# Row maxima from the high halves, four heads in four banks, and an attention order made from a model of bank times

## What is computed

```python
x = L0_attn_X
x = x + 0.5 * _L0_ffn_ref(_layernorm(x, axis=-1), ...)
x = x + _L0_attn_ref(_layernorm(x, axis=-1), ...)
x = x + 0.5 * _L0_ffn_ref(_layernorm(x, axis=-1), ...)
...
scores = jnp.einsum('bhqd,bhkd->bhqk', Q, K) / jnp.sqrt(jnp.float32(D_HEAD))
scores = jnp.where(causal, scores, jnp.float32(-jnp.inf))
A = jax.nn.softmax(scores, axis=-1)
AV = jnp.einsum('bhqk,bhkd->bhqd', A, V)
```

## Time and profile before

| | us |
|---|---|
| median of 3 runs | 2673.28 |
| lowest and highest | 2671.97, 2674.62 |
| span of the profiled execution | 2672.5 |
| attention of batch 0 in it | 774.6 to 1317 |
| attention of batch 1 in it | 1491.3 to 2034 |

### The profile page before, as it was taken

The page is one execution under the profiler, slowest core; times in us unless marked ns, Lnnn a source line. Parts: engine busy times, 40 slices in busy tenths (PEclk is TensorE's granted clock), DMA queues, the critical chain, the costliest instruction groups (busy, mean ns, idle before and its releaser), DMA issues.

```text
span 2672.5 us, 39754 instructions
## 1 busy us (share of the span) xinstructions
PE 2564.6 (96%) x14559; PEld 1350.9 (51%) x14559; DVE 1901.6 (71%) x3387; ACT 1493.0 (56%) x2852; POOL 1513.2 (57%) x1349
## 2 busy tenths in 40 slices
PE   6899999999998999999999999999999999999998
PEld 3555555556773333333478623333335555555554
DVE  7877777767658777777476687777757777776765
ACT  6666666665224666666622245666664466666664
POOL 3466666664323766777332247667773466666665
PEclk9999999999999999999999999999999999999999
DMA  2012211121122020200231310211005201111101
GB/s 64 19 45 97 105 40 48 48 95 48 48 57 59 6 50 6 65 6 3 91 117 32 72 44 9 48 26 45 4 4 201 103 22 43 48 48 48 48 32 48
DMA packets 78018, 136.35 MB, mean 51 GB/s; under 512 B 19551, under 2 KB 24698, under 8 KB 77694
## 3 DMA queue, kind: packets, MB, share of 16 engines
q1 hardware_dynamic: 77822, 133.81, 16.1%
HBM read 71.12 MB, written 34.34 MB: 39 GB/s over the span
## 4 chain that ended last, share of the span: by engine, by line
PE 71%; DVE 12%; POOL 6%; issue 4%; ACT 3%; SPq 1%; DMA 0%; DVEq 0%; POOLq 0%; ACTq 0%
PE pp L95 55%; PE ps L95 15%; DVE sb L116 6%; POOL sb L104 6%; ACT sb L101 3%; DVE sb L110 3%; DVE sb L104 1%; PE ps L98 1%; SPq L137 1%; DVE sb L107 0%; DVE sb L113 0%; PE pp L98 0%; DVE sb L122 0%; DMA sb<-sb 0%; DVE sb L134 0%
## 5 line engine op out<-in xcount | busy, mean ns | idle before, releaser
L95 PE MATMUL pp<-sb,sb 128*128 128x512 f32 (+10 forms) x11128 | 2184.2, 437 | 35.2 <-DVE sb L110 8.5
L104 POOL TENSOR_TENSOR sb<-sb,sb 128x512 f32<-128x512 f32 (+7 forms) x1333 | 1505.6, 1157 | 1143.6 <-ACT sb L101 418.7
L95 PEld LDWEIGHTS pp<-sb,sb 128*32 128x32 f32 (+4 forms) x11128 | 1069.6, 131 | 892.5 <-issue 366.2
L101 ACT ACTIVATE sb<-pp 128x512 f32<-128x512 f32 (+5 forms) x1394 | 666.7, 550 | 425.4 <-PE pp L95 413.9
L95 PE MATMUL ps<-sb,sb 128*128 128x512 f16 (+7 forms) x2888 | 751.4, 348 | 43.1 <-ACT sb L101 14.5
L101 ACT ACTIVATE sb<-sb 128x512 fp32r<-128x512 f32 (+5 forms) x537 | 332.3, 625 | 493.9 <-DVE sb L110 342.7
L116 DVE TENSOR_REDUCE sb<-ps 128x1 f32<-128x512 f32 (+3 forms) x772 | 491.6, 666 | 156.6 <-PE ps L95 154.2
L95 PEld LDWEIGHTS ps<-sb,sb 128*128 128x128 f16 (+4 forms) x2888 | 239.6, 101 | 377.3 <-DVE sb L116 110.9
L110 DVE SCALAR_TENSOR_TENSOR sb<-ps,sb,sb 128x512 f32<-128x512 f32 x437 | 320.3, 747 | 131.6 <-PE ps L95 99.2
L110 DVE SCALAR_TENSOR_TENSOR sb<-pp,sb,sb 128x512 f32<-128x512 f32 x447 | 324.2, 745 | 107.6 <-PE pp L95 104.9
L101 ACT ACTIVATE sb<-pp,sb 128x512 f32<-128x512 f32 x325 | 218.4, 677 | 130.1 <-PE pp L95 115.6
(11 more groups left out here) (27 smaller groups left out, 373.1 us busy)
## 6 DMA issues: line engine op xcount, KB each, us to landing
sb<-sb SPq DMA_DIRECT2D x144, 128.0 KB, 2.4
sb<-L_attn_X SPq DMA_DIRECT2D x64, 256.0 KB, 3.5
sb<-xa SPq DMA_DIRECT2D x64, 256.0 KB, 4.4
sb<-xc SPq DMA_DIRECT2D x64, 256.0 KB, 3.4
xa<-sb SPq DMA_DIRECT2D x32, 256.0 KB, 2.0
xc<-sb SPq DMA_DIRECT2D x32, 256.0 KB, 5.1
out<-sb SPq DMA_DIRECT2D x32, 256.0 KB, 2.0
dd<-sb SPq DMA_DIRECT2D x11, 512.0 KB, 5.3
```

The costliest lines, as they stand in the source:

```text
L95: return self.e.matmul(*a, **k) if self.e else self
L101: return self.e.activation(*a, **k) if self.e else self
L104: return self.e.tensor_tensor(*a, **k) if self.e else self
```

## The change

Four things change. Max units use only the high halves, straight from `p.qs` and `p.ks`: for each head a product of 32 rows, on the partitions that the head has there, into a bank of its own. In the projection part a unit is two heads in banks 0 and 1 and starts from the fifth feature group on; afterwards it is four heads in four banks, each reduced by an instruction of its own, also where few columns are left. The maximum is kept in fp16 alone: `low` and ScalarE's copy are gone, and `combine` writes the fp16 row source. Scores, maxima and rows take banks 0 to 5 from one pool; which one is settled when the order is made, by clocks for TensorE, ScalarE and VectorE that estimate when each bank is cleared. The order of a pair of steps is weigh, maxima, total, scores, weigh, maxima, scores, with zero to two units at each place for maxima. And AV results lie in the other half of their buffer (`av`), since the high halves are read longer.

```diff
@@ Att.max_units
-                    nj = (4, 2, 1, 1)[qb]
-                    units = [(j, 1, ck) for j in range(4) for ck in range(qt)]
-                    units += [(j, nj, qt) for j in range(0, 4, nj)]
...
+                    for ck in range(qt + 1):
                         k0, k1 = 512 * ck, min(512 * ck + 512, 512 * qt + 128 * qb + 128)
...
+                        nj = many[0]
+                        for j0 in range(0, 4, nj):
+                            cnt += nj
+                            yield ("max", hg, qt, qb, ck, j0, nj), k1 - k0
+                            if pend and cnt % 4 == 0:
+                                yield pend.pop(0), 0
@@ Att.order
+            if early:
+                bank = turn % 2
+                turn += 1
+            else:
+                bank = min(range(6), key=lambda i: clear[i])
+                clock["pe"] = max(clock["pe"], clear[bank])
...
-                if g >= 6:
+                if g >= 4:
                     unit()
...
+        def maxima(at):
+            n = 0
+            while n < 2 and spent < total_max * (at + 20) / N:
...
-            while ahead < min(m + (3 if wide else 2), N):
-                scores(ahead)
-                ahead += 1
-            out.append(("weigh", m))
-            if m:
-                self.sum_up(out, parts, m - 1)
-            out.append(("weigh", m + 1))
...
+            for x, k in (('W', 0), ('M', 0), ('T', -1), ('S', 2), ('W', 1), ('M', 1), ('S', 3)):
@@ att_pe, max
-                e.wait_ge(*(t.early if hg == 0 and qt < 3 else t.stacked[i][j]).at((b, hg)))
-                k = e.matmul(bank[:, c0:c0 + w], p.qp[i][0:96, j, q0:q0 + 128], p.kp[i][0:96, j, k0:k1], start=True,
-                             stop=not diag)
...
+            for j in range(j0, j0 + nj):
+                r, bank = slice(32 * j, 32 * j + 32), att_bank_wait(e, p, b, ("max", hg, qt, qb, ck, j))
+                k = e.matmul(bank[:, 0:w], p.qs[r, hg, 0, q0:q0 + 128], p.ks[r, hg, 0, k0:k1], start=True, stop=not diag)
+            if diag:
+                for j in range(j0, j0 + nj):
+                    bank = p.b[t.banks[b].where["max", hg, qt, qb, ck, j]]
+                    k = e.matmul(bank[:, w - 128:w], p.idb[:, :], p.mS[:, :], start=False, stop=True)
             k.then_inc(*t.max_done.up((b, *at)))
@@ att_dve, max
-            e.reduce_max(t.pm[g][:, 4 * qb + j0:4 * qb + j0 + many, ck], x, AX.X).then_inc(*t.max_red.up((b, *at)))
+            for j in range(j0, j0 + nj):
+                e.reduce_max(t.pm[g][:, 4 * qb + j:4 * qb + j + 1, ck], p.b[t.banks[b].where["max", hg, qt, qb, ck, j]][:, 0:w],
+                             AX.X).then_inc(*t.max_red.up((b, hg, qt, qb, ck, j)))
```

## The result

| us | before | forecast | after |
|---|---|---|---|
| median of 9 runs each | 2673.8 | 2617 | 2679.1 |
| span of the profiled execution | 2672.5 | 2616 | 2680.4 |
| weigh 0, batch 0 | 807.8 | 817.5 | 815.9 |
| steps 0 to 19, batch 0, batch 1 | 84.8, 84.8 | 71 | 78.3, 76.9 |
| steps 20 to 139 | 384.7, 384.8 | 357 | 381.5, 381.6 |

The ratio of the medians is 1.0023, with a 95% interval of 1.0013 to 1.0033. The changed kernel is slower, where I had forecast 2.1% faster. The borders of the stretches are the starts of the fp32 records of weigh 0, 20 and 140, counted off as before. Per batch the change made +8.1 (batch 1: +10.7), -6.5 (-7.9), -3.2 (-3.2) and +5.3 (+5.3) us, together +8.6 by these borders. The whole gain was expected in the long stretch, and there it is missing.

A forecast was written before the change was run, and what follows sets the result against it. TensorE was taken as the bound. Per batch, early part +10, steps 0 to 19 -13, long stretch -28 and tail +3 made -28, twice -56: 2617 us from 2673.28, range 2590 to 2645 by itself, 2550 to 2690 with rivals.

The forecast's parts named there:

- Products side by side, 0.22 us a unit: Max units: four 32-row products run together in 0.22 us at 512 columns; long stretch 23 us instead of 87.
- Work and changes of the long stretch, 318 us: Steps 20 to 139, per batch: TensorE's work and tiling changes fall from 349 to 318 us.
- Banks: Long stretch, six shared banks: a full pair waits about 0.5 us; waits 36 plus 3, stretch 357 us instead of 385.
- what is late next: Long stretch engine totals: VectorE 280 us, GpSimd 270, ScalarE 235; TensorE at 318 still leads by little.
- The forecast's last line: Failure signs: a unit over 0.4 us, early turn-round far from 0.57 us, or TensorE waiting for GpSimd's adds before each total.
- Steps 0 to 19, -13: First 20 attention steps, per batch: VectorE and TensorE loads both close, so 71 us instead of 84.7.
- Early part +10: Before weigh 0: two-head units wait for both reductions, 1.84 us per 512 columns; weigh 0 at 817.5 instead of 807.8 us.
- Tail +3: From step 140: second fp32 runs cost 2.2 us and the rows chain stalls 2, less a 1.24 us wait removed.
- TensorE's clock: Attention stretches: clock read as 1.00 in all four, the 2.4 GHz level.
- Weight loads in a row: Rival, chance 0.20 with banks: four loads make a unit 0.40 us, not 0.22; 26 us per batch, 2669 us in all.
- Better cover: Rival, chance 0.17: six shared banks cover waits as in the tail; long stretch near 332 us, 2550 us in all.
- no overlap: Rival, chance 0.12: 32-row products run one after another, 0.87 us a unit; 54 us per batch more, 2781 us in all.

The follow-up runs named there:

- a run with the same 20 steps: Changed kernel with the splits of output weights and first AV quarter moved to the last 17 steps; 2664.0 us, 0.9964 of the kernel before.
- the best kernel: Changed kernel with single signals per head, splits moved to the end, and two-head units in steps 0 to 19; 2640.3 us, 0.9877 of the kernel before.

## Why the forecast was wrong, step by step

- **Products side by side, 0.22 us a unit: right**, and measured (the second four 0.22 us after the first).
- **Work and changes of the long stretch, 318 us: right** (318.0). The changes alone cost 46.6 us, 15.1 before; 45 were priced. (The 51 diagonal units of the prediction are 48 in the order, under 1 us.)
- **The step that failed** is the wait term at the end of "Banks": "So waits do not shrink with the work: I keep 36 and add 3". It priced the waits of all 60 pairs from a walk through one full pair. They measured 63.5 us, not 39. The full pair was right (6.02 us, 0.53 of waits), but 24 pairs wait 1.5 us on the mean, 0.9 to 2.5 each, and take 16 us more than in the kernel before. In 15 of them VectorE has more to do than TensorE, since TensorE's part is short beside the diagonal while the reductions are full, and since the reciprocals lie between them. "TensorE (318) still leads, by little" compared sums over 385 us; it should have been compared pair by pair. Halving the reductions takes 19 us of the 63.5 away, 14 of them in these 24 pairs; what holds the rest of their waits is open.
- **Not in the sum at all**: GpSimd's row of twelve operations at step 136, some 8 us a batch, and so about a third of the 24.5 us; 8.7 and 11.8 us of the long stretch went when they were moved. The sentence on what is late next kept GpSimd's total at 270 and did not look where its splits stand. The forecast's last line named a wait for GpSimd's adds as what would make it fail; it came in one pair above all.
- **Steps 0 to 19, -13: half right** (-6.5, -7.9). Work and changes were 53.9 of the 56 priced; waits of 24.5 us, for banks and for VectorE, were taken as 15. Some 4 us of batch 0's are the low clock's (74.3 us in a run with the same 20 steps).
- **Early part +10, measured +8.1 and +10.7: right**. The cause shows in the trace: units of 512 columns start 1.8 to 2.0 us apart (800.68, 802.44, 804.41), 1.84 was priced, and TensorE's waits for reductions there are 19 us instead of 4. **Tail +3, measured +5.3**: changes of tiling +1.9, waits +3.2.
- **TensorE's clock** was taken as 1.00. Its granted clock in five short stretches of the changed kernel:

```profile
core 0: us, PE busy (x) PEld busy (x) DVE busy (x) ACT busy (x) POOL busy (x), PEclk, DMA share, GB/s
824.00:831.00 7.00, 6.62 (x33) 1.30 (x33) 5.93 (x12) 1.05 (x4) 1.69 (x4) 0.51 0.95 217
831.00:834.00 3.00, 2.63 (x22) 0.85 (x20) 1.16 (x4) 2.22 (x5) 0.00 (x0) 1.00 0.35 87
834.00:838.00 4.00, 3.84 (x13) 0.71 (x13) 3.34 (x7) 2.15 (x4) 0.00 (x0) 0.57 0.00 0
848.00:851.40 3.40, 3.31 (x15) 0.52 (x14) 1.98 (x4) 1.76 (x4) 0.26 (x1) 0.50 0.08 22
1261.00:1268.00 7.00, 6.29 (x25) 1.06 (x26) 0.07 (x1) 2.06 (x4) 5.56 (x5) 0.51 0.00 0
```

  0.51 is the 1.2 GHz level. It stands for 27 us of batch 0's attention and 20 of batch 1's, behind the early part with its waits for banks and behind the 4.7 us at 1257; in the attention of before there was none. The same ten steps with and without such a place, in the two batches, differ by 0.4 to 1.6 us, so for the six to eight of them I estimate 3 to 13 us a batch; the best kernel, with fewer waits there, shows 1.00 throughout batch 0's attention. That the waits bring the low clock fits the runs (with five banks and 107 us of waits it lasts 55 us in batch 0, with one run of fp32 groups and 109 us of waits 44); it was not tested apart.
- **The rivals.** "Weight loads in a row" gave 2669 also for waits of 1.0 us a pair; they were 1.06. It was the nearest, with the tail and the clock on top. Its own mechanism is refuted, since a unit costs 0.22 us and not 0.40, and the walk's 0.5 us for a full pair stood; the waits came from other pairs, so that the nearness is in part luck. Better cover, 2550, was taken from a tail without maxima and is refuted; no overlap is excluded.

What stays open: what holds the long pairs at 20, 24 and 46, and the larger half of the long pairs' waits, which stays with short reductions; what moving the splits is worth in the kernel before; and what the early part would cost with a third bank, which was not tried.

## What to carry to other kernels

Where engines are within a fifth of each other, compare their work group by group of the loop, not over the stretch: the waits come from the groups in which another engine leads for a moment, and in which small jobs that are rare in the sum stand in a row. A change that shares buffers and asks for several at once needs its waits priced for every kind of group, including those with side work. And when one engine is made faster, look for the places where the others' side work had just been covered: moving it paid here (the run with the splits moved is 15 us faster, and its two long stretches are 8.7 and 11.8 us shorter), while the change as a whole gave nothing.

## What was not expected of the hardware

- Two 32-row products side by side take as long as four, 0.22 us for 512 columns each; half-filled units cost 22.6 us a batch in the run with two heads a unit.
- A change between row tiles, column tiles and full products costs about 0.1 us each way, whichever two of them it is (0.09 to 0.13, priced here as 0.105). 444 such changes are 46.6 us a batch where 144 were 15.1; the difference is half of the 65 us that the small products free.
- TensorE's clock fell to 1.2 GHz for stretches of 3 to 7 us while its products show it busy for most of the time (6.62 of 7 us at 824), in a kernel whose page shows TensorE at 94%.
